# Turning the attention probabilities by DMA instead of on TensorE, and weighing V two steps later

## The reference

```python
x = x + attn(layernorm(x), Wq, bq, Wk, bk, Wv, bv)
x = x + ffn(layernorm(x), weight, scale_weight, bias)   # y @ (weight * scale[:, None]).T + bias

# attn: 16 heads of 64
q, k, v = (split_heads(x @ W + b) for W, b in ...)
# block i of 128 queries sees keys [128 i - 64, 128 i + 192)
ctx = softmax(q_block @ k_window.T / 8) @ v_window
idx = [0] + top_62_tokens_by_norm(q) + [1023]           # per head
ctx[idx] = softmax(q[idx] @ k.T / 8) @ v                # over all 1024 keys
```

## Time and profile before

| | us |
|---|---|
| median of 3 runs | 2138.94 (2134.4 to 2142.42) |
| the profiled execution's own time | 2139.94 |
| its span, first to last instruction | 2138.4 |
| granted TensorE clock, mean | 0.998 |
| from the first attend of a batch to the last (8 pairs) | about 331 |
| one pair | 41.4 |

### The profile page before, as it was taken

One profiled execution on the slowest core, in us unless ns is written; L12 is line 12 of the kernel. 1 busy time (PEld: TensorE's weight loads), 2 busy tenths in 40 slices (PEclk: granted clock), 3 DMA queues, 4 the chain that ended last, 5 costly groups with the idle time before them and its releaser, 6 DMA issues.

```text
span 2138.4 us, 36665 instructions
## 1 busy us (share of the span) xinstructions
PE 2105.3 (98%) x12576; PEld 1794.5 (84%) x12576; DVE 1347.3 (63%) x2615; ACT 750.6 (35%) x1915; POOL 502.7 (24%) x336
## 2 busy tenths in 40 slices
PE   6999999999999999999999999999999999999999
PEld 6878888888788888887888888888888888888887
DVE  5686666546966665459656655496555566666664
ACT  4334344442344344432444445224434451000000
POOL 2231121123411221243112311432123112212121
PEclk9999999999999999999999999999999999999999
DMA  4333232223332322233322221323223113333331
GB/s 161 104 95 92 75 104 67 61 69 99 107 90 75 106 60 65 69 95 93 98 85 77 84 70 42 103 65 86 65 68 123 51 58 134 140 131 134 137 128 69
DMA packets 192506, 194.29 MB, mean 91 GB/s; under 512 B 91984, under 2 KB 157590, under 8 KB 192400
## 3 DMA queue, kind: packets, MB, share of 16 engines
q1 hardware_dynamic: 184752, 175.19, 27.7%
q10 hardware_dynamic: 4320, 15.73, 1.8%
q0 software_dynamic: 3328, 2.17, 0.6%
HBM read 122.73 MB, written 51.44 MB: 81 GB/s over the span
## 4 chain that ended last, share of the span: by engine, by line
PE 85%; DVE 11%; issue 2%; DMA 1%; ACT 1%; DVEq 0%; SPq 0%; POOL 0%; ACTq 0%; POOLq 0%
PE proj L566 40%; PE proj L742 15%; PE pv L691 10%; PE score L664 5%; PE turn L679 5%; PE pv L722 3%; DVE top_idx L1307 2%; DVE x_norm L1309 2%; PE score L704 2%; DVE top_val L1305 2%; DVE q_sq L1272 2%; PE turn L714 1%; PE turn L731 1%; PE proj L831 1%; DVE norms L1274 1%
## 5 line engine op out<-in xcount | busy, mean ns | idle before, releaser
L566 PE MATMUL proj<-xT_hi,w_lo 128*128 128x512 f32 x1536 | 409.6, 398 | 0.0
L566 PE MATMUL proj<-xT_hi,w_hi 128*128 128x512 f32 x1536 | 402.7, 404 | 2.5 <-issue 1.5
L566 PE MATMUL proj<-xT_lo,w_hi 128*128 128x512 f32 x1536 | 381.5, 390 | 0.0
L434 POOL CAST w_hi<-w_raw 128x1024 fp32r<-128x1024 f32 x96 | 100.7, 1049 | 1178.4 <-PE proj L566 910.3
L566 PEld LDWEIGHTS proj<-xT_lo,w_hi 128*128 128x128 f32 x1536 | 288.6, 188 | 63.1
L566 PEld LDWEIGHTS proj<-xT_hi,w_lo 128*128 128x128 f32 x1536 | 281.1, 188 | 62.2 <-issue 0.2
L566 PEld LDWEIGHTS proj<-xT_hi,w_hi 128*128 128x128 f32 x1536 | 274.2, 188 | 63.4 <-DVE kT_lo L1290 2.7
L994 ACT ACTIVATE probs<-score,neg_max 128x256 f32<-128x256 f32 (+1 forms) x512 | 229.2, 460 | 183.4 <-DVE neg_max L1363 122.5
L691 PEld LDWEIGHTS pv<-v_nat,pT 128*128 128x128 f32 x2048 | 248.1, 191 | 10.4
L691 PE MATMUL pv<-v_nat,pT 128*128 128x64 f32 x2048 | 242.3, 271 | 0.0
L436 POOL TENSOR_TENSOR w_lo<-w_raw,w_hi 128x1024 fp32r<-128x1024 f32 x96 | 232.4, 2421 | 7.8
(11 more groups left out here) (165 smaller groups left out, 2975.0 us busy)
## 6 DMA issues: line engine op xcount, KB each, us to landing
w_raw<-in_wstream SPq DMA_DIRECT2D x96, 512.0 KB
x_buf<-in_rows SPq DMA_DIRECT2D x55, 512.0 KB, 4.1
q_rows<-q_nat SPq DMA_DIRECT2D x64, 256.0 KB
ctx_rows<-ctx_out SPq DMA_DIRECT2D x128, 128.0 KB, 1.8
q_store<-ctx_rows SPq DMA_DIRECT2D x30, 512.0 KB
out<-q_store ACTq DMA_DIRECT2D x30, 512.0 KB, 2.6
q_store<-in_cols SPq DMA_DIRECT2D x28, 512.0 KB
q_store<-in_rows SPq DMA_DIRECT2D x8, 512.0 KB, 5.3
```

The costliest lines, as they stand in the source:

```text
L434: pool.tensor_copy(w_hi[b][:, :], w_raw[b][:, :]).then_inc(w_hi_set, 1)
L566: mm = pe.matmul(proj[:, bank, :], w[b][:, k * P:k * P + P], x[:, k, half * HALF:half * HALF + HALF], start=(m == 0), stop=(m == 23), skip ...
```

## The change

What it does:

- `turn_p`, `turn_gp`, `p_out` and `gp_out` are gone. DVE's new `part_p` copies one half (one head, 512 words) of `probs` into two 2-byte planes, SP's `turn_p` issues a transposing DMA on it (1024 2-byte columns; the last half of the global one has 1280), and ACT's `join_p` puts the words together in `pT`. That is 10 copies, 10 DMAs and 10 copies a pair.
- The PSUM tensor `turn` is free then, so scores go alternately to `score` and `turn` (`score_of`). `pT` has two buffers and a third, `pT_g`, for the global ones; `probs` has one, and `exps` now waits until `part_p` has read it.
- `weigh` of a step comes after the scores of the step two later; the last two of a pair (`weigh(u, 3)`, `global_weigh(u)`) move into the next pair.
- Both halves of V are projected in front of K (`part_of`: "vvkk"; in pair 6 "vkvk"), and a token half now picks the PSUM bank (`seat`). In before V always went to bank 0 and K to bank 1.
- V is turned in 3 pieces of 3 tiles (768 columns each) instead of 2, its source planes share `q_sq`, and `join_v` moves from DVE to ACT. `v_out` is one instruction a half instead of two for the first.
- Small moves: places of the column work, the first pairs' `early_q_out`, the loads for the first two tiles of the linear layer, the bias load, and a wait inside the first projection part of the last pair.

```diff
@@ PE
-            def turn_p(u, s):
-                for h in range(2):
-                    pe.wait_ge(exp_set, 2 * (u * EVENTS + s) + h + 1)
...
-                            mm = pe.transpose(turn[0:rows, col:col + P], probs[:, src:src + rows], ident[:, :])
-                    mm.then_inc(p_turned, 1)
             def weigh(u, s):
                 pe.wait_ge(pv_free, u * EVENTS + s + 1)
-                if s < 2:
-                    pe.wait_ge(v_set, 2 * u + s + 1)
+                pe.wait_ge(v_set, u * V_PIECES + V_PIECES + V_NEEDS[s])
                 for h in range(2):
-                    pe.wait_ge(pT_set, 2 * (u * EVENTS + s) + h + 1)
+                    pe.wait_ge(pT_set, u * (2 * EVENTS) + 2 * s + h + 3)
...
+            def attend(n, hp):
+                scores(n, hp, 0)
+                part_of(n, hp, 0)
+                if not opens:
+                    weigh(u - 1, 3)
+                part_of(n, hp, 1)
+                scores(n, hp, 1)
+                if not opens:
+                    global_weigh(u - 1)
+                part_of(n, hp, 2)
+                scores(n, hp, 2)
+                part_of(n, hp, 3)
+                weigh(u, 0)
+                part_of(n, hp, 4)
+                scores(n, hp, 3)
+                turn_gq(u)
+                part_of(n, hp, 5)
+                weigh(u, 1)
+                if not early:
+                    part_of(n, hp, 6)
+                global_scores(u)
+                weigh(u, 2)
...
@@ SP
+            def turn_p(n, hp, s):
+                i = n * (PAIRS * EVENTS) + hp * EVENTS + s
+                for h in range(2):
+                    words = half_words(s, h)
+                    sp.wait_ge(p_parted, 2 * i + h + 3)
+                    apart(sp)
+                    sp.wait_ge(pT_set, 2 * i + h + 1)
+                    apart(sp)
+                    sp.dma_start_transpose(p_turned[:, 2 * words.start:2 * words.stop].rearrange("p (x r) -> p x r", r=P),
+                                           p_parts[:, 2 * words.start:2 * words.stop]).then_inc(p_moved[h], 16)
@@ ACT
+            def join_p(n, hp, s, h):
+                act.wait_ge(p_moved[h], 16 * i + 32)
...
+                act.copy(pT_of(s)[:, words].bitcast(U16).rearrange("p (x s) -> p s x", s=2),
+                         p_turned[:, 2 * words.start:2 * words.stop].rearrange("p (s x) -> p s x", s=2)).then_inc(pT_set, 1)
...
+                exps(u, 3, 0)
+                gq_hi_out(u)
+                before(3, 0)
+                exps(u, 3, 1)
+                before(3, 1)
+                if not last:
+                    out("v", 1, 2)
@@ DVE
+            def part_p(n, hp, s, h):
+                dve.wait_ge(exp_set, 2 * i + h + 3)
+                dve.wait_ge(p_moved[h], 16 * i + 16)
+                apart(dve)
+                dve.tensor_copy(p_parts[:, 2 * words.start:2 * words.stop].rearrange("p (s x) -> p s x", s=2),
+                                probs[:, words].bitcast(U16).rearrange("p (x s) -> p s x", s=2)).then_inc(p_parted, 1)
```

More of the change, by code:

```diff
@@ L330, in stores @@
             def stores(n, hp, next_slices, following):
+                last = hp == PAIRS - 1
                 if next_slices:
@@ L1055, in attend, with out @@
-                columns(3)
-                if last:
-                    out(1, 0)
-                gq_hi_out(u)
-                p_out(u, 3)
-                columns(4)
+                def out(what, h, b):
+                    if not last:
+                        (v_out if what == "v" else k_hi_out)(n, hp + 1, h)
+                    elif following:
+                        early_q_out(n + 1, b % 2, b // 2)
+                exps(u, 0, 0)
+                before(0, 0)
+                if ahead:
+                    ahead_hi(1)
@@ L1064, in attend @@
                 global_exps(u)
-                columns(5)
-                out(0, 1)
-                gp_out(u)
-                columns(6)
-                out(1, 1)
-                if last and not following:
-                    lin_hi(0, 0)
+                for h in range(2):
+                    join_p(n, hp, STEPS - 1, h)
+                columns(4)
+                if early and not following:
+                    ahead_hi(0)
+                out("k", 1, 3)
+                if last:
+                    if ahead:
+                        lin_hi(0, 0)
+                    for h in range(2):
+                        join_p(n, hp, STEPS, h)
+                    if following:
+                        act.wait_ge(pv_done, u * EVENTS + STEPS)
@@ L1459, in attend @@
                 u, last = n * PAIRS + hp, hp == PAIRS - 1
+                ahead = last and not following
                 def top_norms(k):
@@ L1482, in attend @@
+                part_p(n, hp, 0, 0)
                 if ahead:
                     ahead_lo(1)
-                join_v(u, 1)
-                maxima(u, 1)
+                if hp > 0:
+                    pv_out(u - 1, 3)
+                part_p(n, hp, 0, 1)
                 inverses(u, 0)
                 top_norms(1)
+                if not last:
+                    columns(0)
+                maxima(u, 1)
+                if hp > 0:
+                    g_out(u - 1, hp - 1)
+                part_p(n, hp, 1, 0)
@@ L1596, in batch @@
                 top_find(n, 1, 2)
-                part_v(n, 0, 1)
+                for k in range(1, V_PIECES):
+                    part_v(n, 0, k)
                 k_lo_out(n, 0, 1)
```

736 lines of the change are left out of this document (411 added, 325 removed).

## The result

The changed kernel takes 2243.84 us (median of 4 runs, 2241.47 to 2247.68) against 2138.02 for the kernel before, measured beside it: 1.0496 of before, interval 1.047 to 1.0521. It is slower by 5%, where I forecast 2028 us and faster.

The account below looks back on a forecast made before the run. PE was taken as the bound. From 2139.9 us, 144 saved, 29 back for the `v_out` stall and 4 for batch edges give 2029; less 1 us to the median, 2028. The 8 in 10 range was 1997 to 2080.

Parts of the forecast that it names:

- What bounds it: In the attends only PE's own work sets the pace: busy for all 41.4 us of a pair, at full clock.
- what PE loses: Transposes leaving PE make 4.6 us a pair, taken as 4.5; a pair without wait 36.9 us, 32 pairs save 144.
- What the others get: Per pair: DVE 26.4 to 30.5 us, ACT 17.4 to 24.8, DMA engines 25.3 of 37; SP's issues 17.
- the upper bound of 1.30: Highest price in us for ACT's `join_p` of 1024 elements, from DVE paying 23% more for interleaved writes; 1.06 taken.
- DVE's fast row: `part_v` at 685 ns for 1024 elements, about two a cycle; used to price nine probability copies at 0.69 us each.
- The DMA rival: DMA engines become the bound from 2.6 us per 1000 columns; 2221 us at 2.8, 2303 at 3.0; chance 0.09.
- The stall at `v_out`: PE waits 1.2 us before part 6 for bank 1, freed late by ACT, in 24 pairs: 29 us back.
- The edges: At each batch's first and last pair, 1 us added per batch, 4 us in all.

Follow-up runs that it names:

- e5: Changed kernel with e4's edits, at most one load or half of the statistics' store between two turning DMAs, first statistics' roots one step earlier still: 2128 us.
- e3: Changed kernel with ACT's write of V^T's second half (`v_out`) ahead of step 3's exponentials in pairs 0 to 5: 67 us less than the changed kernel.
- e7: e5 with the statistics' stores issued by ACT in pair 3 and the column load moved ahead of the weight load: 2097.5 us, 0.9806 of before.
- e8: e5 with two added 512 KB DRAM-to-DRAM copies per pair that nobody waits for: 25.5 us more than e5.
- e10: e7 with the next batch's row loads and last column put back between the second and third turning DMA: 40 us more than e7.
- e2: Changed kernel with statistics' roots two steps earlier in pair 3, their store behind the fourth turning DMA, spreading loads at pair 3's end: 17 us less.
- e9: e7 with the second half of V^T written behind step 3's exponentials again, as in the changed kernel: 44 us more than e7, 2141.84 us.
- e4: Changed kernel with row loads behind the turning DMAs, statistics two steps earlier and `v_out` ahead of step 3's exponentials: 80 us less than the changed kernel.

## Why the prediction was wrong

**What bounds it, what PE loses: right.** 4.3 us a pair, 41.4 to 37.1 (4.5 forecast).

**What the others get: right but for one size.** DVE 29.8 us a pair (30.5), DMA 25.2 us of engine time a pair, 0.68 of 37.1 in e5 (25.3). `join_p` took 1.36 us, not 1.06, and above the upper bound of 1.30; that bound used a mean of 845 ns which four slow copies of 32 had raised (median 0.76 us), so that it came as near as it did is luck. e3 shows that this alone costs little: with the joins as dear as they are the pairs ran at 37.1 in the last batch. DVE's fast row held for the new shape: the median copy of 1024 takes 0.69 us. The Trainium skill ("VectorE: DVE Perf Modes", section "Mode 2×_2P — use both read ports for one tensor") says that a copy in SBUF moves two elements a cycle when its outermost dimension is even; the trace agrees, with 0.69 us for 1024 elements in two halves. The page allows an odd one too, where it is equal in source and destination; the copy of 1280 before the change is written with 5 tiles in both and took 1.49 us, so that part is not borne out here. The mean is 0.81 because 18 of the 288 copies take 2.1 to 2.9 us. Every one of the 18 runs beside an elementwise instruction of POOL and ends 0.55 us after it, as here; of the 262 quick ones (up to 0.75 us) one shares more than 0.3 us with POOL's `w_lo`, and 13 with its shorter `w_hi`. No run moved POOL's work, so what it costs the kernel is not shown.
```profile
309.40 2.60 POOL L502 TENSOR_TENSOR w_lo<-w_raw,w_hi 128x1024 fp32r<-128x1024 f32 x1
...
309.65 2.90 DVE L1496 COPY p_parts<-probs 128x1024 uint16<-128x1024 uint16 x1
```

**The DMA rival: wrong as stated.** The engines did not become the bound of a pair (e7, e8), except perhaps around the statistics' store, where e7 shows them at 1.21. I had given slower 0.09 on that mechanism alone, and slower came by another.

**The step that failed** is the sentence on SP: "SP's loads of 512 KB stand in the same queue between the transposing DMAs; two of them at a pair's start delay step 0 by some 3 us, inside its room", and behind it "Neither is the bound at this price". I priced SP by the sum of its issues, as one does with a transfer engine, and never walked down its order: I did not ask of each load ahead of a turning DMA what it waits for and when that comes. Against e7 that order costs 40 us for the row loads and the last column alone (e10). The other part is the stretch at the statistics, 57 us in three batches against undisturbed pairs, of which e2 gave back 10 us an interval and lost 2 to 4 again in the one ahead. Taken together: e9 has the changed kernel's place of `v_out` and everything else of e7 (SP's order, the statistics' roots earlier, their store on ACT's queue) and takes 2141.84 us, so these are worth 102 of the 216 us by which the forecast missed.

**The stall at `v_out`: place, count and mechanism right, its size wrong.** In the changed kernel it is 79.9 us of waits for 29. Nine of the 24 waits, in pairs 0 to 2 of the first three batches, make 57 us there and 11 in e9: that excess is SP's delay. The other 15 make 23 us, 1.5 each for the forecast 1.2. A second term comes out once SP's order is right. "ACT starts its first exponential 0.83 us after the scores" was read in a pair where DVE had nothing else in front of step 3's maxima; in pairs 3 to 5 of e9 it is 3.4 to 5.0 us, and 41 of its 58 us of waits stand there. Of this the columns' scaling in pairs 4 and 5 is in the changed kernel too, where its waits are 1.1 and 2.3 to 2.7 us; the roots in pair 3 are not.

**Where the 216 us between forecast and measurement stand**, counted from the distances above with 38.4 us as the undisturbed pair: 55 us in the first three intervals of three batches, 57 in the interval from 3 to 4, 13 from 4 to 7, 26 in the last batch, of which 20 in the last pair, where four loads of 512 KB stand ahead of the third turning DMA and its first half lands 9.0 us after its issue; 15 in the first opening, 25 in the three turnovers, and some 21 because the forecast was 0.3 us a pair shorter and had put a gain on openings too. That makes 212; the profiled execution was 2.4 us quicker than the median. Part of each is the clock: 0.95 as a mean in the changed kernel, 0.98 in e7. Of the 114 us by which e9 stands above the forecast, 50 are between pairs 2 and 5 of the first three batches, 9 in the first opening and 15 in the turnovers.

**The edges: wrong.** I put 1 us on each batch; the first opening lost 15.2 us (from 27.8 to 42.9, first scores to global scores). SP's order and `v_out` give back 9 of them (e7, 34.0); the rest is not explained.

## What to carry to other kernels

When a change puts a latency-bound transfer into a queue that also has bulk loads, write down that queue's order as one does for a compute engine: for each entry what it waits for, when that comes, how long it occupies the queue, and which of the transfers behind it is needed next. Do the same for the engine that starts the chain: what else stands in its order ahead of the instruction that the late one waits for, in every pair and not only in the one that you read. A load that waits for an engine's later work belongs behind the last transfer that this engine's present work needs, and bulk loads go one by one into the gaps. Moving the slow store of small pieces to another queue did not shorten the stretch around it (3-4 and 4-5, e5 against e7). The share of the DMA engines says nothing about it: the slow pairs had the lower share.

## What the runs showed of the hardware

- A copy of 1024 2-byte elements on ACT from SBUF to SBUF that interleaves two planes took 1.36 us, and 1.08 for 768 elements; the fp32 copy of 1024 had been 1.06.
- Two stores of 1024 statistics each in 4-byte pieces, issued 0.57 us apart, landed 9.9 and 10.9 us after their issue in the changed kernel (medians of three), both 11.3 in e4.
- After 6.8 us of waiting the granted clock was 0.50 and stayed there for the whole next part (window 278.14:282.00 of the changed kernel); in a pair with a wait of 1.06 us it was 1.00 (e9, last batch).
- The slow ones among DVE's copies of probabilities, 1024 elements in over 1.5 us, all run beside an elementwise instruction of POOL and end 0.55 us after its end: 18 of 18 in the changed kernel, 19 of 19 in e7, 10 of 10 in e9.
- The statistics' store on ACT's queue did not stop the turning on SP's, but it did not leave it alone either: in e7 the engines were at 1.21 of the window 295 to 300 us while moving 46 GB/s, and DVE's wait for the turned V was 6.50 us (12.73 in e4, with the store in SP's queue). The Trainium skill ("DMA: Bandwidth & Descriptors", section "Queues, rings and completion order") says that each DMA engine takes turns between queues, packet by packet. The trace fits that, but no run isolates it, since e7 moved other transfers too.
